# A four-layer transformer block on one core: order of the steps planned forwards and backwards, and the first MLP chunk worked on batch by batch

## The reference

```
L0, L1, L2:  shift, scale, gate (two sets of three) = split(silu(c) @ w_ada + b_ada, 6)
             x = x + gate_a * proj(attention(LN(x) * (1 + scale_a) + shift_a))   16 heads of 18
             x = x + gate_m * mlp(LN(x) * (1 + scale_m) + shift_m)               288 -> 1152 -> 288
L0's mlp:    4 experts, all computed; logits = xn @ w_gate, softmax over the top 2 of 4 gives
             the weights cw (0 for the others); sum over experts of cw[e] * (gelu(xn @ w1[e] + b1[e]) @ w2[e] + b2[e])
L1:          attention of each token among its own 16 heads (scores 16 x 16 per token), exact gelu
L0, L2:      attention among the 256 tokens of a batch, per head; tanh gelu
L3:          U = Q factor of P (288 x 64); R = expm(skew matrix of silu(c) @ W.T + b) per batch
             x = x + (x U R - x U) U^T
```

## Time and profile before

| | us |
|---|---|
| median of 3 runs | 1387.23 |
| profiled execution, its own time | 1388.27 |
| its span, first to last instruction | 1386.1 |
| TensorE (PE) busy | 1296.8 (94%) |
| VectorE (DVE) busy | 899.0 (65%) |
| ScalarE (ACT) busy | 784.3 (57%) |
| GpSimd (POOL) busy | 444.5 (32%) |

### The profile page before, as it was taken

One profiled execution on the slowest core, in us unless ns is written; L12 is line 12 of the kernel. 1 busy time (PEld: TensorE's weight loads), 2 busy tenths in 40 slices (PEclk: granted clock), 3 DMA queues, 4 the chain that ended last, 5 costly groups with the idle time before them and its releaser, 6 DMA issues.

```text
span 1386.1 us, 33182 instructions
## 1 busy us (share of the span) xinstructions
PE 1296.8 (94%) x13225; PEld 946.5 (68%) x13225; DVE 899.0 (65%) x1983; ACT 784.3 (57%) x1565; POOL 444.5 (32%) x817
## 2 busy tenths in 40 slices
PE   5687999999999899999998999899998999999998
PEld 3343756777777688777887778787675767676775
DVE  5787887767686574666537654675665855776454
ACT  3665558677666342455337344666454676756653
POOL 4122425335243432323433333223331314231210
PEclk9788999999999999999999999999999999999999
DMA  8413154554543323232324323322000020000001
GB/s 232 114 31 73 38 145 115 141 143 121 144 98 70 89 58 86 32 69 94 94 49 75 69 57 123 99 41 66 5 14 2 14 56 3 14 6 15 2 29 52
DMA packets 81935, 96.20 MB, mean 69 GB/s; under 512 B 40077, under 2 KB 74998, under 8 KB 78454
## 3 DMA queue, kind: packets, MB, share of 16 engines
q1 hardware_dynamic: 81510, 93.79, 27.5%
q10 hardware_dynamic: 272, 0.29, 0.1%
HBM read 73.22 MB, written 16.38 MB: 65 GB/s over the span
## 4 chain that ended last, share of the span: by engine, by line
PE 74%; DVE 12%; issue 5%; ACT 3%; DMA 3%; POOL 3%; SPq 1%; DVEq 0%; POOLq 0%; ACTq 0%
PE P L1577 18%; PE P L1424 12%; PE P L1587 7%; PE P L1589 7%; PE P L1588 7%; DVE NM L1845 5%; PE P L1553 4%; PE P L1544 2%; PE P L1520 2%; PE P L1451 2%; DMA QT<-MT 1%; PE P L1441 1%; PE P L1598 1%; PE P L1464 1%; PE P L1584 1%
## 5 line engine op out<-in xcount | busy, mean ns | idle before, releaser
L1577 PE MATMUL P<-XT,W 128*128 128x256 f16 x3024 | 351.5, 273 | 6.6 <-ACT FULL L2106 3.6
L1577 PEld LDWEIGHTS P<-XT,W 128*128 128x128 f16 x3024 | 289.8, 98 | 57.0 <-issue 12.6
L2285 POOL TENSOR_TENSOR X<-X,TM 128x288 f32<-128x288 f32 x144 | 124.3, 865 | 497.6 <-DVE TM L1920 352.4
L1587 PE MATMUL P<-W,H 128*128 128x288 f16 x864 | 247.5, 286 | 0.0
L1589 PE MATMUL P<-W,H 128*128 128x288 f16 x864 | 247.1, 286 | 0.0
L1588 PE MATMUL P<-W,H 128*128 128x288 f16 x864 | 247.1, 286 | 0.0
L2192 ACT ACTIVATE G<-P 128x512 f32<-128x512 f32 (+1 forms) x240 | 133.2, 555 | 171.7 <-PE P L1577 163.2
L2181 ACT ACTIVATE ARENA<-P 128x512 f32<-128x512 f32 x256 | 135.1, 599 | 72.7 <-PE P L1544 72.1
L1845 DVE TENSOR_REDUCE NM<-P 128x2 f16<-128x512 f32 x256 | 159.5, 686 | 11.8 <-PE P L1529 11.4
L1424 PE MATMUL P<-WQ,XT 128*128 128x288 f16 x1008 | 145.6, 296 | 11.3 <-DVE XT L1756 5.1
L2290 POOL TENSOR_TENSOR H<-G,H 128x512 f16<-128x512 f32 (+1 forms) x97 | 105.7, 1095 | 128.5 <-ACT H L2193 126.2
(11 more groups left out here) (304 smaller groups left out, 2132.8 us busy)
## 6 DMA issues: line engine op xcount, KB each, us to landing
W<-scr_w SPq DMA_DIRECT2D x9, 1440.0 KB, 6.2
W<-scr_w SPq DMA_DIRECT2D x9, 1368.0 KB, 6.0
scr_w<-W SPq DMA_DIRECT2D x4, 1440.0 KB, 5.9
scr_w<-W SPq DMA_DIRECT2D x4, 1368.0 KB, 5.8
STG<-in_L_w SPq DMA_DIRECT2D x8, 576.0 KB, 4.8
STG<-in_L_w SPq DMA_DIRECT2D x9, 432.0 KB, 3.4
STG<-in_L_WT SPq DMA_DIRECT2D x11, 324.0 KB, 4.4
G<-scr_ada SPq DMA_DIRECT2D x24, 144.0 KB, 3.0
```

The source lines that it names most:

```text
L1577: ins = e.matmul(bank(st)[:, 256 * k:256 * k + 256], W1[:, w, m * 128:(m + 1) * 128], XT[:, x, at:at + 256], start=i == 0, stop=i == 6)
L1587: e.matmul(o, hi, W2[:, 2 * m, :], start=False, stop=False)
L2285: e.tensor_tensor(X[:, t, :], X[:, t, :], TM[st["k"]][:, :], ALU.add).then_inc(st.sem)
```

## The change

There are two changes and what they need. First, `improved` takes the place of the single call of `by_readiness`. It plans forwards as before, then from the end (`from_the_end`: each engine's steps reversed, each step after those that depend on it), and sets `st.index` to minus the time from the step's beginning to the end of that reversed plan. The next forward plan takes this as the rank among steps that can begin within 0.1 us. This is done six times (`TIMES`), and of the six forward plans the one with the smallest TensorE clock by the estimates is kept. Second, `SPLIT` has an entry for layer 0's chunk 0: its todo entries are (expert 0, batch 0), (expert 0, batch 1), (expert 1, batch 0) and so on. An entry's up and down products follow each other for one batch. `gates` is called with tiles t0 to t1, for chunk 0 twice with two tiles, for the others once with four.

```diff
-SPLIT = {(2, 3): [(0,), (1,)]}
+SPLIT = {(0, 0): [(0,), (1,)], (2, 3): [(0,), (1,)]}
+TIMES = 6
...
-            st.index, st.end = k + 100000 * (st.kind in LATE), None
+            st.end = None
...
-        st.end = lands(st, lane.clock)
+        st.end, st.done = lands(st, lane.clock), lane.clock
         lane.steps.append(st)
+
+def from_the_end(lanes):
+    queues, then, late = [], {}, {}
+    for lane in lanes:
+        some = {}
+        for st in reversed(lane.steps):
+            name = "table" if st.kind in TABLES else id(st.sem)
+            some.setdefault(name, deque()).append(st)
+            for x in st.deps:
+                then.setdefault(id(x), []).append(st)
+        queues.append(list(some.values()))
+    clocks = [0.0] * len(lanes)
+    while True:
+        best = None
+        for k, some in enumerate(queues):
+            mine = None
+            for qu in some:
+                if qu and all(id(x) in late for x in then.get(id(qu[0]), [])):
+                    st = qu[0]
+                    begin = max(clocks[k], max((late[id(x)] + LAT + st.end - st.done for x in then.get(id(st), [])), default=0.0))
+                    key = (begin if begin > clocks[k] + NEAR else clocks[k], -st.done)
+                    if mine is None or key < mine[0]:
+                        mine = key, begin, qu
+            if mine and (best is None or mine[1] < best[0]):
+                best = mine[1], k, mine[2]
+        if best is None:
+            return
+        begin, k, qu = best
+        st = qu.popleft()
+        clocks[k] = late[id(st)] = begin + st.cost
+        st.index = -clocks[k]
+
+def improved(lanes, lands, wire):
+    for lane in lanes:
+        for k, st in enumerate(lane.steps):
+            st.index = k + 100000 * (st.kind in LATE)
+    best = None
+    for _ in range(TIMES):
+        wire.clock = 0.0
+        by_readiness(lanes, lands)
+        if best is None or lanes[0].clock < best[0]:
+            best = lanes[0].clock, [list(lane.steps) for lane in lanes]
+        from_the_end(lanes)
+    for lane, steps in zip(lanes, best[1]):
+        lane.steps, lane.clock = steps, best[0]
...
-        xt_ones = do(pool, "xt_ones", 5.5, incs=7)
+        xt_ones = do(pool, "xt_ones", 5.5, incs=7, after=consts)
...
-        def gates(c4):
-            lg = [tok["lg", t] for t in range(4 * c4, 4 * c4 + 4)]
-            top = do(dve, "g_top", 0.45, incs=2, c=c4, lg=lg, free=tok.get("cw"))
-            x = do(act, "g_exp", 0.25, c=c4, src=top)
-            tok["cw"] = [do(dve, "g_mix", 2.3, incs=11, c=c4, lg=lg, src=x)]
+        def gates(t0, t1):
+            lg = [tok["lg", t] for t in range(t0, t1)]
+            top = do(dve, "g_top", 0.45, incs=2, t0=t0, t1=t1, lg=lg, free=tok.get("cw"))
+            x = do(act, "g_exp", 0.25, t0=t0, t1=t1, src=top)
+            tok["cw"] = [do(dve, "g_mix", 2.3, incs=11, t0=t0, t1=t1, lg=lg, src=x)]
...
-                    if L == 0 and (c, "cw") not in self.done:
-                        self.done.add((c, "cw"))
-                        gates(c)
+                    if L == 0 and (c, vs) not in self.done:
+                        self.done.add((c, vs))
+                        gates(4 * c + 2 * vs[0], 4 * c + 2 * vs[-1] + 2)
...
-        wire.clock = 0.0
-        by_readiness([pe, dve, act, pool, sp], lands)
+        improved([pe, dve, act, pool, sp], lands, wire)
...
-                e.tensor_reduce(L1[:, :], l3, AX.X, ALU.max).then_inc(st.sem)
+                e.tensor_reduce(L1[:, 0:n], l3, AX.X, ALU.max).then_inc(st.sem)
```

More of the change, by code:

```diff
@@ L1873, in gate_views @@
             def gate_views(st):
-                return [LG[:, 4 * st["c"]:4 * st["c"] + 4, :], CWA[:, 4 * st["c"]:4 * st["c"] + 4, :], CWM[:, :, :]]
+                t0, t1 = st["t0"], st["t1"]
+                return t1 - t0, LG[:, t0:t1, :], CWA[:, t0:t1, :], CWM[:, 0:t1 - t0, :]
             def g_top(st):
-                l3, CW, _ = gate_views(st)
+                n, l3, CW, _ = gate_views(st)
                 q.wait_ge(st["lg"], st["free"])
-                e.tensor_reduce(L1[:, :], l3, AX.X, ALU.max).then_inc(st.sem)
+                e.tensor_reduce(L1[:, 0:n], l3, AX.X, ALU.max).then_inc(st.sem)
                 q.wait_ge(st.at(1))
-                e.tensor_tensor(CW, l3, L1[:, :].unsqueeze(2).broadcast_to([128, 4, NE]), ALU.subtract).then_inc(st.sem)
+                e.tensor_tensor(CW, l3, L1[:, 0:n].unsqueeze(2).broadcast_to([128, n, NE]), ALU.subtract).then_inc(st.sem)
             def g_mix(st):
[L1884 to L1888, removed]
+                n, l3, CW, CWS = gate_views(st)
+                e4 = l3.unsqueeze(3).broadcast_to([128, n, NE, NE])
+                j4 = l3.unsqueeze(2).broadcast_to([128, n, NE, NE])
+                t4 = LT[:, 0:n, :].rearrange("p t (e j) -> p t e j", e=NE)
+                m4 = LM[:, 0:n, :].rearrange("p t (e j) -> p t e j", e=NE)
                 q.wait_ge(st["lg"])
@@ L1892, in g_mix @@
                 q.wait_ge(consts, st.at(2))
-                e.tensor_tensor(LM[:, :, :], LM[:, :, :], TRI[:, :].unsqueeze(1).broadcast_to([128, 4, 16]), ALU.mult).then_inc(st.sem)
+                e.tensor_tensor(LM[:, 0:n, :], LM[:, 0:n, :], TRI[:, :].unsqueeze(1).broadcast_to([128, n, 16]), ALU.mult).then_inc(st.sem)
                 q.wait_ge(st.at(3))
-                e.tensor_tensor(LT[:, :, :], LT[:, :, :], LM[:, :, :], ALU.add).then_inc(st.sem)
+                e.tensor_tensor(LT[:, 0:n, :], LT[:, 0:n, :], LM[:, 0:n, :], ALU.add).then_inc(st.sem)
                 q.wait_ge(st.at(4))
@@ L1902, in g_mix @@
                 q.wait_ge(st.at(7))
-                e.tensor_reduce(L1[:, :], CW, AX.X, ALU.add).then_inc(st.sem)
+                e.tensor_reduce(L1[:, 0:n], CW, AX.X, ALU.add).then_inc(st.sem)
                 q.wait_ge(st.at(8))
-                e.reciprocal(L1[:, :], L1[:, :]).then_inc(st.sem)
+                e.reciprocal(L1[:, 0:n], L1[:, 0:n]).then_inc(st.sem)
                 q.wait_ge(st.at(9))
-                e.tensor_tensor(CW, CW, L1[:, :].unsqueeze(2).broadcast_to([128, 4, NE]), ALU.mult).then_inc(st.sem)
+                e.tensor_tensor(CW, CW, L1[:, 0:n].unsqueeze(2).broadcast_to([128, n, NE]), ALU.mult).then_inc(st.sem)
                 q.wait_ge(st.at(10))
@@ L2183, in g_exp @@
             def g_exp(st):
-                CW = CWA[:, 4 * st["c"]:4 * st["c"] + 4, :]
+                CW = CWA[:, st["t0"]:st["t1"], :]
                 q.wait_ge(st["src"])
```

## The result

The changed kernel took 1365.18 us (median of 4 runs, 1364.5 to 1368.9) against 1387.97 for the kernel before on the same chips: ratio 0.9843, 95% interval 0.9821 to 0.9865, 22.8 us less. The prediction was 1364. The experiments show that this agreement hides two wrong terms of opposite sign, so the profile is read here first for where the time went, and only then for why.

A forecast was written before the change was run, and what follows sets the result against it. It took TensorE, busy 1296.8 of 1386.1 us, as the bound. Terms 6 + 2 + 9 + 5 + 2.3 - 1 = 23.3 us won gave 1364 us, own range 1352 to 1376, 8-in-10 range 1346 to 1385.

The forecast's parts named there:

- the hole at 34: TensorE from 34 to 52 us: ranking batch 1's transposes and projections earlier wins 6 us (4.5 idle, 1.5 clock).
- The lower bound: For 34 to 52 us: nothing is won if the transposes' two banks come free only behind the maxima.
- Rest of the first 100 us: Idle outside 34 to 52 us and not for first data: the order wins 2 of 9.8 us.
- Batch 0 early: From 100 to 144.3 us: batch 0's early expert 0 work wins 5 us idle and 2.3 clock; costs charged at 1.
- The rival on the weights' cover: First chunk: reloads of W1 and W2 lose 42 us of cover, making the kernel slower, 1396 us; chance 0.12.
- Behind 144 us: Short TensorE waits after 144.3 us: the order wins a fifth, 9 of 44.9 us of idle.
- Householder and tables: Householder chain ranked behind the rest, contained in the 6 us; ten more table loads at most, within the 1 us charged.
- the forecast's 0.55: Chance the prediction gave its own forecast of 1364 us, with a range from 1352 to 1376.

The follow-up runs named there:

- e10: e1 with batch 1's first LN, transposes and XT columns in layer 0 dealt right behind batch 0's; 1347.7 us, ratio 0.9705.
- e1: The changed kernel without the batch-wise first chunk, so only the order planned from the end; 1352.7 us, ratio 0.9727.
- e2: The changed kernel with one plan only, so the batch-wise first chunk with the order as dealt; 1416.4 us, ratio 1.0182.
- the other deal: BIAS 0.25 instead of 0.2 when lines are dealt: the changed kernel took 1363.5 us with it, e1 1367.8 us.
- e3: The kernel before with the Householder chain's steps ranked last among those that can begin within 0.1 us; 1386.0 us, ratio 0.9971.
- e4: e2 with layer 0's experts 1 to 3 on expert 0's W1 and W2, so no reloads there; 1406.0 us, ratio 1.0126.
- e5: The kernel before with layer 0's experts 1 to 3 on expert 0's W1 and W2, so no reloads there; 1402.7 us, ratio 1.0102.
- e6: The changed kernel with only expert 0 of the first chunk batch by batch, experts 1 to 3 taking both batches; 1362.2 us, ratio 0.9807.
- e12: e1 with BIAS at 0.25 instead of 0.2, which only changes how lines are dealt; 1367.8 us, ratio 0.9818.
- e9: e1 with the rank from the end for all engines but TensorE, which keeps the dealt rank; 1368.3 us, ratio 0.9854.

## Why the prediction was right in the sum and wrong in two steps

The prediction named its own signs. These came: idle from 100 to 144 of 6.0 (4 to 7 named), idle behind 240 us down from 39.0 to 27.8 (near 31), a later last Householder step, and no wait for W among the largest. These failed: TensorE busy 10.1 us from 34 to 52 (12 or more), batch 1's transposes at 38.8 (before 35), a clock of 0.85 from 100 to 144 (above 0.9), and the first up product at 126.6 (102 to 115). That the hole at 34 stays was one of the three things by which it would call itself wrong, and the hole stayed. Term by term:

- **The hole at 34 (6 us taken).** Failed: busy 10.1 of 18 and clock 0.62 against 8.2 and 0.61, so 1.9 of the 4.5 us of idle and nothing of the clock; the transposes moved with the rest. The lower bound, "if the two banks of the transposes come free only behind the maxima", was what happened, and e10 showed it. That batch 1's rows had been ready for 20 us was read as a matter of rank; it was a buffer.
- **Rest of the first 100 us (2).** The whole of the first 100 gave 2.8 of idle and about 2.4 of clock (66.9 x 0.14 = 9.4, now 69.7 x 0.10 = 7.0): 5.2 for the 8 of both terms. Most of the idle came where the prediction expected none: of the 13.5 us until the first weights and the first normalised batch, 11.6 are left (one wait). Batch 0's normalised rows are ready at 13.9 instead of 17.8, since GpSimd's factors for them (RS) let ScalarE begin at 12.8 instead of 16.7.
- **Batch 0 early (7.3, less 1).** The idle time from 100 to 144.3 fell by 5.3, as taken, but only a half of it by the split: the order alone brought 2.6 (e1 has 8.7), the split alone 2.0 (e2 has 9.3), the split beside the order 2.7. The 2.3 of clock didn't come (0.84 before, 0.85 after). And this gain of 2 to 3 us was more than lost from 200 to 400. In all the split was not a gain of 6.3 but a cost of 16 beside the order (25 alone); in the other deal it was neither. The rival on the weights' cover named the place, and the lag that the traces show there; it had a chance of 0.12, since "the same stretch was 94% busy" was said of a stretch in which whole chunks gave the cover.
- **Behind 144 us (9).** The idle time there fell from 44.9 to 34.5, by 10.4, and that this is near 9 is luck: the order alone took 20.5 of it (24.4 left in e1), and the split gave 10.1 back. So nearly a half went and not a fifth. The argument for a fifth was that the plan's gaps are partly accidents of its estimates; but the planner's own clock fell by 32.7 us for e1 where the chip gained 38, so most of the gain was in the plan.
- **Householder and tables.** About 4 us for the chain's rank (e3). Four more table loads in the changed kernel; e4, with eight more than e5 and one more gate, is 3 us slower.

So the order is the term that was mis-sized (17 taken, 38 to 47 measured) and the split the one with the wrong sign (6 gained taken, 16 to 25 lost measured); 47 - 25 is the 22 that came out. That the sum was right is luck: two wrong terms cancelled, and the forecast's 0.55 was right by its number only.

The version that the experiments point to is e10: the order, the first chunk whole, and batch 1's transposes dealt early. It is 1.4% below the changed kernel.

What stays open: why the split costs 16 to 25 us in one deal and nothing in another, what e6 lost against e1 although its reloads had their cover, why the order gains more beside the split (47 against 38), and how much of e12's clock loss is the kernel's and how much the run's. Reloads made cheaper in the changed kernel itself, with ranks from the end, weren't tried.

## What to carry to other kernels

When one change has two parts, cost each as if it came alone, and look in its neighbour's stretch for the cover that both count on: with a reload's cover halved TensorE had 10 to 21 us more of idle from 200 to 400 us, while the trace of before showed the stretch full. A wait that lasts 20 us behind ready data is first a question of which buffer, and only then of rank. And a plan made by list scheduling moves by 28 us when one constant moves by 0.1: try a variant in more than one deal before its cost is called its own, compare on the chip, and take the planner's clock for large differences only.

## What the runs showed of the hardware

TensorE's busy time isn't a fixed quantity: 13225 matmuls took from 1285.7 us (e10) to 1304.6 (e2) by the page's first part. Their mean granted clocks were 0.986 and 0.973; by busy x (1-g) that is an estimated 18.0 and 35.2 us lost, 17 of the 19 between them. The clock doesn't simply follow the idle time: from 100 to 144.3 us the changed kernel was idle for 6.0 us at a clock of 0.85, e9 for 9.5 at 0.96.

One kernel's runs differ in the same way: the six of e12 took 1360.8 us at a mean clock of 0.987 up to 1369.5 at 0.979. So a few us between two profiled runs can be the clock of the run and not the order of the steps.

First e2, then e10:

```profile
PE 1304.6 (92%) x13225; PEld 950.4 (67%) x13225; DVE 906.0 (64%) x2003; ACT 791.5 (56%) x1577; POOL 419.3 (30%) x803
```

```profile
PE 1285.7 (96%) x13225; PEld 944.0 (70%) x13225; DVE 905.0 (67%) x1985; ACT 781.0 (58%) x1557; POOL 449.5 (33%) x823
```
